# Attention's row maxima taken in query order, without their transpose, and the experts' sum and the division's loads cut into pieces

## What is computed

```python
# attention of the second layer: 4 batches x 16 heads, 2048 positions, head size 16
a1 = softmax(einsum('bhnd,bhmd->bhnm', q1, k1) * scale); x1 = a1 @ v1      # heads 0 to 7
a2 = softmax(einsum('bhnd,bhmd->bhnm', q2, k2) * scale); x2 = a2 @ v2      # heads 8 to 15
s = concatenate([x1 - lv * x2, x2], -1) @ Wp.T + bp
# experts of the second layer, two for each token
gathered = exp_out[flat_e, minimum(pos_safe, cap - 1)]
f = segment_sum(where(keep, gates_f, 0.0)[:, None] * gathered, tok)
out = x + s * silu(f)
```

## Time and profile before

| | us |
|---|---|
| median of 3 runs | 4986.67 (4985.71 to 4993.23) |
| the profiled execution's own time | 5028.41 |
| its span | 5026.6 |
| DVE busy | 4272.8 (85%) |
| PE busy | 4415.5 (88%) |
| ACT busy | 3679.6 (73%) |
| POOL busy | 1542.7 (31%) |

### The profile page before, as it was taken

One profiled execution on the slowest core, in us unless ns is written; L12 is line 12 of the kernel. 1 busy time (PEld: TensorE's weight loads), 2 busy tenths in 40 slices (PEclk: granted clock), 3 DMA queues, 4 the chain that ended last, 5 costly groups with the idle time before them and its releaser, 6 DMA issues. The chain is left out here.

```text
span 5026.6 us, 91334 instructions
## 1 busy us (share of the span) xinstructions
PE 4415.5 (88%) x33129; PEld 1757.9 (35%) x33129; DVE 4272.8 (85%) x5013; ACT 3679.6 (73%) x6260; POOL 1542.7 (31%) x1014
## 2 busy tenths in 40 slices
PE   6768777778776699999899998999999999999998
PEld 3225225225223355566322222222222222222225
DVE  5997997898897366555799998999998999999996
ACT  5765775676673333334699998999998999989992
POOL 1982993893795200000011111211110311130003
PEclk8998998999998799999999999999999999999998
DMA  2402101201202322221111112111112211222116
GB/s 80 160 1 101 35 1 68 67 1 47 71 1 71 105 84 72 69 88 55 39 36 35 36 40 51 48 39 35 41 40 40 53 35 41 52 53 63 29 23 189
DMA packets 302467, 275.38 MB, mean 55 GB/s; under 512 B 167924, under 2 KB 264015, under 8 KB 299407
## 3 DMA queue, kind: packets, MB, share of 16 engines
q1 hardware_dynamic: 264748, 166.27, 12.1%
q0 software_dynamic: 32128, 100.57, 6.7%
q10 hardware_dynamic: 5202, 3.18, 0.3%
HBM read 150.17 MB, written 118.69 MB: 53 GB/s over the span
## 5 line engine op out<-in xcount | busy, mean ns | idle before, releaser
L1787 DVE TENSOR_REDUCE at_mpart<-at_ps 128x1 f32<-128x1024 f32 x2048 | 2352.5, 1212 | 99.9 <-PE at_ps L1676 65.3
L1772 ACT ACTIVATE at_E<-at_ps 128x512 f32<-128x512 f32 x4096 | 2222.2, 594 | 178.3 <-PE at_ps L1691 89.6
L1698 PE MATMUL at_ps<-at_E,at_vst 128*32 128x256 f32 x16400 | 1317.0, 393 | 26.0 <-ACT at_osb L1753 21.8
L1676 PE MATMUL at_ps<-at_ks,at_qs 48*128 48x512 f16 x4096 | 801.8, 388 | 51.7 <-DMA at_qs<-at_mrow 26.0
L1691 PE MATMUL at_ps<-at_qs,at_ks 50*128 50x512 f16 x4096 | 792.3, 383 | 29.1 <-ACT at_E L1772 27.3
L1560 POOL DMA_INDIRECT at_y<-yd,at_gidx x128 | 129.8, 1014 | 1680.1 <-DVE at_mx L1792 1630.0
L887 POOL TENSOR_TENSOR l_work<-l_work 128x1024 f32<-128x1024 f32 x252 | 594.2, 2358 | 34.0 <-issue 0.9
L783 PE MATMUL l_ps<-l_bc,l_sel 96*128 96x512 bf16 x1024 | 319.8, 397 | 249.0 <-DVE l_work L921 124.8
L1698 PEld LDWEIGHTS at_ps<-at_E,at_vst 128*32 128x32 f32 x16400 | 326.8, 108 | 566.3 <-issue 414.4
L1676 PEld LDWEIGHTS at_ps<-at_ks,at_qs 48*128 48x128 f16 x4096 | 196.3, 92 | 874.2 <-DVE at_mpart L1787 447.5
L819 PE MATMUL l_ps<-l_work,l_ident 128*128 128x512 f32 x1024 | 490.1, 601 | 5.1 <-DVE l_work L921 5.1
(11 more groups left out here) (269 smaller groups left out, 4129.1 us busy)
## 6 DMA issues: line engine op xcount, KB each, us to landing
xd<-l_zero SPq DMA_DIRECT2D x4, 5120.0 KB, 32.9
yd<-at_late POOLq DMA_DIRECT2D x40, 512.0 KB, 3.0
at_late<-xd POOLq DMA_DIRECT2D x38, 512.0 KB, 4.9
at_qs<-qp SPq DMA_DIRECT2D x132, 128.0 KB
at_ks<-kp SPq DMA_DIRECT2D x396, 32.0 KB
at_late<-in_eW SPq DMA_DIRECT2D x8, 1536.0 KB, 8.3
ot<-at_osb SPq DMA_DIRECT2D x516, 17.0 KB
at_qs<-qp SPq DMA_DIRECT2D x132, 64.0 KB
```

What stands on the lines that cost most here:

```text
L1676: mm = pe.matmul(ring[n % 2][:, r, :], m.qs[row, buf, bass.ts(i, P)], m.ks[row, buf, bass.ts(kh, BANK)], start=True, stop=True)
L1698: mm = pe.matmul(O[32 * q:32 * q + 32, :], m.vst[:, par, SLOTS_A * kk + sl, :], m.E[:, sl % 4, kk, bass.ts(q, QG)], start=(sl == 0 and kk ...
L1772: act.activation(m.E[:, sl % 4, kk, bass.ts(hf, BANK)], S[chunk(sl, 2 * hf + kk) % 3], ACT.Exp, scale=scale).then_inc(s.ex, 1)
L1787: dve.tensor_reduce(m.mpart[:, job:job + 1], ring[n % 2].rearrange("p a b -> p (a b)"), AX_X, ALU.max).then_inc(s.ring_free, 1)
```

## The change

Three things change.

1. **Query order.** `peak` takes as its 128 weights every eighth query of the half (`peak_queries`), so that partition p holds queries 8p to 8p+7 and `mx` read by partitions is in query order. The transpose, its turn in the score banks, `mneg` and its scaling go; ScalarE scales `mx` straight into the high part (128 x 8), VectorE makes the low part with one operation, and the DMA into the row under the queries reads 8 elements (16 bytes) from each of 128 partitions instead of 128 elements (256 bytes) from each of 8.
2. **Places.** `mpart` has two halves; `last` of a step moves behind the first maximum of the next step, where nothing waits for it at once. `high_row` stands at the end of slot pair 1, `low_row` after the eighth maximum, `copy_out` before the fourth exponential instead of behind it. In `run_experts` the second half's fold and transpose go.
3. **Pieces.** The store of a part's sum becomes four DMAs of 128 KB, issued between the next part's gathers, and the two loads of 1024 KB become eight of 256 KB, one with each gather of the next part.

```diff
+def peak_queries(m, row, buf, i):
+    half = slice(i // 8 * QB, (i // 8 + 1) * QB)
+    return m.qs[row, buf, half].rearrange("r (p i) -> r i p", i=8)[:, i % 8, :]
...
+    def store_piece(done, i):
+        b, part = done // PARTS, done % PARTS
+        pool.dma_start(io.f[b:b + 1, :, part, i * D:(i + 1) * D].rearrange("o p n -> (o p) n"), m.fsum[:, i, :]).then_inc(m.moved, 16)
+        moved[0] += 16
...
+                    if done and n % 2 == 0:
+                        store_piece(done - 1, i)
+                    if done - 1 in LOAD_BEHIND:
+                        load_piece(LOAD_BEHIND.index(done - 1), n)
...
-            pool.dma_start(io.f[b:b + 1, :, part, :].rearrange("o p n -> (o p) n"),
-                           m.fsum.rearrange("p i d -> p (i d)")).then_inc(m.moved, 16)
             if done in LOAD_BEHIND:
-                load_heads(LOAD_BEHIND.index(done))
+                load_sums(LOAD_BEHIND.index(done))
...
-                for k in range(KD):
-                    pool.dma_start(m.nT[:, b, k, :], io.ot[h0 + 8 * k:h0 + 8 * k + 8, 0:HD, :].rearrange("h c t -> h c t")).then_inc(m.n_in, 16)
+            def load_piece(b, n):
+                h0, k, cols = b * H1 + 1, n // 4, bass.ts(n % 4, BANK)
+                pool.dma_start(m.nT[:, b, k, cols], io.ot[h0 + 8 * k:h0 + 8 * k + 8, 0:HD, cols].rearrange("h c t -> h c t")).then_inc(m.n_in, 16)
...
-                    mm = pe.matmul(ring[n % 2][:, r, :], m.qs[row, buf, bass.ts(i, P)], m.ks[row, buf, bass.ts(kh, BANK)], start=True, stop=True)
+                    mm = pe.matmul(ring[n % 2][:, r, :], peak_queries(m, row, buf, i), m.ks[row, buf, bass.ts(kh, BANK)], start=True, stop=True)
...
-                pe.transpose(S[TURN_CHUNK % 3][0:8, 0:P], m.mx[:], m.ident[:]).then_inc(s.turned, 1)
...
-                act.activation(m.mneg[:], S[TURN_CHUNK % 3][0:8, 0:P], ACT.Identity, scale=-(2.0 ** -ROW_EXP)).then_inc(s.ex, 1)
-                act.wait_ge(s.ex, drained(t, TURN_CHUNK))
+            def high_row(t):
+                act.wait_ge(s.mfin, t + 2)
                 act.wait_ge(s.mrow, ROW * (t + 1))
-                act.copy(m.mrow[:, 0, :], m.mneg[:]).then_inc(s.mhi, 1)
+                act.activation(m.mrow[:, 0, :], m.mx[:], ACT.Copy, scale=-(2.0 ** -ROW_EXP)).then_inc(s.mhi, 1)
...
-                dve.tensor_tensor(m.mrow[:, 1, :], m.mneg[:], m.mrow[:, 0, :], ALU.subtract).then_inc(s.mlo, 1)
+                dve.scalar_tensor_tensor(m.mrow[:, 1, :], m.mx[:], -(2.0 ** -ROW_EXP), m.mrow[:, 0, :], ALU.mult, ALU.subtract).then_inc(s.mlo, 1)
...
-                dve.wait_ge(s.mfin, t + 2)
+                dve.wait_ge(s.mfin, t + 1)
                 for sl in range(SLOTS_A):
                     for kh in range(2):
-                        peak(2 * sl + kh, PRO + local, PRO + NRING * t + local + 1)
+                        peak(2 * sl + kh, half, PRO + local, PRO + NRING * t + local + 1)
+                        if local == 0:
+                            dve.wait_ge(s.mlo, t + 1)
+                            last(1 - half, PRO + NRING * t)
                         local += 1
                     if sl == LOW_AT:
                         low_row(t)
-                last(PRO + NRING * t + local)
```

More of the change, by code:

```diff
@@ L1099 @@
 ROW = 64 * 1
-ATT_SEMS = "init loaded v_loaded v_free score ex av o_copy o_st0 o_st1 ring ring_free mfin turned mneg mhi mlo mrow"
+ATT_SEMS = "init loaded v_loaded v_free score ex av o_copy o_st0 o_st1 ring ring_free mfin mhi mlo mrow"
 def load_rows(eng, io, m, n):
@@ L1392, in _ @@
                         weights_high(e + 1)
[L1393 to L1397, removed]
+                    if n == HIGH_AT:
+                        act.wait_ge(a.mfin, 1)
+                        act.activation(m.mrow[:, 0, :], m.mx[:], ACT.Copy, scale=-(2.0 ** -ROW_EXP)).then_inc(a.mhi, 1)
             @block.vector
@@ L1569, in combine_experts @@
             pool.wait_ge(m.summed, done + 1)
-            pool.dma_start(io.f[b:b + 1, :, part, :].rearrange("o p n -> (o p) n"),
-                           m.fsum.rearrange("p i d -> p (i d)")).then_inc(m.moved, 16)
             if done in LOAD_BEHIND:
-                load_heads(LOAD_BEHIND.index(done))
+                load_sums(LOAD_BEHIND.index(done))
             if done in DIVIDE_BEHIND:
                 divide(DIVIDE_BEHIND.index(done))
-    pool.wait_ge(m.moved, MOVED * PARTS * B)
+    for i in range(FT):
+        store_piece(PARTS * B - 1, i)
+    pool.wait_ge(m.moved, moved[0])
 def attend(nc, io, m, s):
@@ L1690, in scores @@
                     row = slice(64 * r, 64 * r + STACK + 2)
-                    mm = pe.matmul(S[(l + r) % 3], m.ks[row, j, bass.ts(sl, P)], m.qs[row, j, half * QB + hf * BANK:half * QB + (hf + 1) * BANK],
+                    mm = pe.matmul(score_bank(t, l + r), m.ks[row, j, bass.ts(sl, P)], m.qs[row, j, half * QB + hf * BANK:half * QB + (hf + 1) * BANK],
                                    start=True, stop=True)
@@ L1729, in step @@
                         values((sl - 1) % SLOTS_A, hf, (j if half or sl else j + 1) % 2)
-                        if sl == TURN_AT and hf == 0:
-                            turn(t)
                 assert local == NRING
@@ L1771, in step @@
                         for kk in range(2):
-                            act.activation(m.E[:, sl % 4, kk, bass.ts(hf, BANK)], S[chunk(sl, 2 * hf + kk) % 3], ACT.Exp, scale=scale).then_inc(s.ex, 1)
-                        if sl == TURN_AT and hf == 0:
-                            turn(t)
+                            if (sl, hf, kk) == COPY_AT:
+                                copy_out(t, par, pairs)
+                            act.activation(m.E[:, sl % 4, kk, bass.ts(hf, BANK)], score_bank(t, 4 * sl + 2 * hf + kk), ACT.Exp, scale=scale).then_inc(s.ex, 1)
+                    if sl == HIGH_AT:
+                        high_row(t)
             for t in range(2 * HEADS):
```

75 lines of the change are left out of this document (30 added, 45 removed).

## The result

The changed kernel takes 4902.2 us (median of 4 runs, 4897.3 to 4908.6), the kernel before 4986.2 in the same comparison (4978.0 to 4993.2): a ratio of 0.9833, 95% interval 0.9814 to 0.9852, about 84 us less. The forecast was 4907 us, with a chance of 0.78 for faster.

A forecast was written before the change was run, and what follows sets the result against it. Three engines within 1.3 us of each other were taken to bound the step, none alone. 52 us from shorter steps and 28 from long waits made 80, so 4986.7 - 80 = 4907 us, range 4878 to 4990.

The forecast's parts named there:

- The transfers: Store and loads cut into pieces in attention: two long waits around `mrow` go, 15.7 + 12.5 = 28 us; bounds 0 and about 40.
- The step: One quiet attention step falls from 19.01 to 18.60 us, 0.41 less, over 127 steps 52 us.
- wrong by B: Sign set for the new profile: TensorE slots of 1.14 to 1.17 us would speak for rival B.
- x: Extra time of a strided peak weight-load pair, likely added to TensorE's slot; taken as 0.015 us, upper bounds 0.047 and 0.10.
- rival B: TensorE becomes the bound but not badly, x 0.03 to 0.06, steps 18.75 to 18.95, 4926 to 4951 us; chance 0.23.
- half of float32's cost a column: Upper bound for the strided peak load: float16's quickness lost, half of float32 a column paid, x = 0.047 us.
- Fold and low part: VectorE's small operations in a step, 0.20 us each beside 18.08 of maxima, so a floor of 18.48.
- What three close engines cost each other: Step taken as 18.60 us, over the highest floor of 18.48, since three close engines do not run at it.
- The copy's place: Copy ahead of ScalarE's fourth exponential: still costs 0.31 us, a ready exponential stands behind it; wait for values 0 to 0.3.
- turning point: Where the stride makes the change slower: a TensorE slot of 1.183 us, x = 0.073.
- rival C: The stride decides: strided pair costs as float32, x = 0.10, slot 1.21, 5042 us, slower; chance 0.16.
- D: Rival: transfers gain nothing, `mrow` still held in two or three steps, only the step's 52 us gained, 4935 us; chance 0.05.

The follow-up runs named there:

- the two halves: Only the pieces put into the kernel before: 4950.7 us, ratio 0.9945; the changed kernel with the old bursts of store and loads: 4932.1 us, ratio 0.9899.

## Why the prediction was right

**The transfers** were right in mechanism and size: 28 us forecast, 29 with the pieces alone, 34 of folds' excess in the whole. The long waits need the large loads issued together with `mrow`, as the runs of the two halves show. The order has a share that the prediction did not give it: with the old bursts it already took away one of the two waits. That pieces and `mrow` do not meet was argued from their times in a step, and no wait for `mrow` is left.

**The step** was right in size, 18.60 forecast and 18.64 measured, but by luck and not by the sum's terms. Of the signs that the prediction set itself, the peak loads (140 ns, not 92 to 110) and the slots (1.157, "wrong by B") went against it:

- *x, the strided load, was mis-sized*: 0.015 us taken, 0.048 measured. The pair begins only when the values have streamed, as the prediction read from the earlier trace rows, so all of it came on the slot, 1.157 us instead of 1.125, and TensorE became the bound. That is rival B's mechanism, though not its time: 16 x 1.157 and the 0.3 that B put at the seam are 18.81 us and about 4933, and the seam cost 0.13. (B's own range is also narrower than its terms: 18.3 to 18.7 and 0.3 give 18.6 to 19.0.) The estimate from half of float32's cost a column, 0.047, which I had only as a bound, hit it. The Trainium skill's rule on 16-byte lines (SBUF — State Buffer, "SBUF cachelines") had the direction, and the trace agrees with it: 92 and 93 ns within 4 bytes, 140 at 16 and no more at 32. By that page two accesses to a line suffice, and there the runs differ: 109 ns at 8 bytes. The other reading in the prediction, that at this step between columns the load stays near 92 ns, did not hold either.
- *Fold and low part were taken too dear*: 0.20 each, 0.07 and 0.08 measured. VectorE's floor is 18.25, not 18.48. In the kernel before it was read too low, 18.77 instead of 18.85, since the last maximum ahead of the fold counts in full, 1.21 and not 1.13.
- *ScalarE was taken as never idle but for 0.35 us.* Its 0.562 for an exponential held small waits. It was idle for 1.03 us of that step, and the earlier trace rows have 178.3 us over 128 steps, 1.39 each. Its floor in the changed kernel is by estimate near the 17.73 us that it is busy there, not 18.42.
- *What three close engines cost each other, 0.12, is not there*: with contiguous weights the step is VectorE's floor.
- *The copy's place was under-read.* The prediction put the 0.35 us of ScalarE's wait down to VectorE's pause at the seam. The runs show a second holder, TensorE's values waiting for the copy: putting the copy back loses 0.31 us a step in the changed kernel, putting the fold back only 0.06. The copy alone gave 0.19 in the kernel before, and there the fold's wait held the rest. The view of waits behind the earlier trace rows had this holder, 21.8 us in 76 waits, and the prediction did not use it.

The prediction had VectorE highest and TensorE lowest of the three; measured, TensorE holds the step and ScalarE lies lowest. The floors of VectorE and ScalarE too dear, TensorE's 18.0 too cheap and the 0.12 on top met near the right sum. By the prediction's own turning point rival C, slower, lay only 0.073 - 0.048 = 0.025 us of load away; by the measured gain, an estimate, 84 us over 127 x 16 slots, it was 0.041.

**Rivals.** C asked for x of 0.073 in the changed kernel; in the kernel before, with the transpose and the old copy, 0.047 was already enough for 43 us. D did not happen.

## What to carry to other kernels

When a change gives a matmul's weights a stride, look at what stands ahead of the load: behind a matmul of 512 columns it was covered, behind the short ones it lengthened each of the 2048 slots by its full 0.047 us. Of those 96 us only 40 were to be had back, since VectorE's floor comes next. Where several engines are within a few per cent, find for each the wait that holds it and who holds the holder; a wait at a seam may have two causes, and taking away one shows little. Small DMAs on which a step depends should not be issued together with megabytes that could as well be spread or sent behind them. And a timeline's merged rows hide short waits: before an engine is called never idle, its busy time over the step is to be held against the step.

## What was not expected of the hardware

Weight loads of 128 float16 columns took 92, 93, 109, 140 and 139 ns at 2, 4, 8, 16 and 32 bytes from column to column. Four small DMAs issued at the same time as 2.5 MB from another queue held TensorE until some 23 us later: SP began to issue them at 3033.59 us and TensorE's wait of 14.8 us ended at 3056.55. Just ahead of it VectorE's low part took 1.68 us instead of 0.16 and ended at 3033.57, with POOL's sum, which ended at 3033.54; so `mrow` and the burst left together. What held the low part was not tested. Small operations on 128 x 8 elements hold VectorE for 0.07 us between long ones, though one takes 0.16.
